# Moving the expansion and mask transfers of a weight-reconstruction stage from ScalarE's DMA queue to GpSimd's

## The reference, cut to what matters

```python
n = out_size * in_size                      # 16.8 million samples
p0, p1, p2, p3 = (control_points[idx[k]] for k in range(4))
w = 0.5 * (2*p1 + (p2-p0)*f + (2*p0-5*p1+4*p2-p3)*f2 + (3*p1-p0-3*p2+p3)*f3)
x = x + ln(attention(ln(x)))
x = x + ln((silu(ln(x) @ gate_w.T) * (ln(x) @ up_w.T)) @ down_w.T)
```

## Time and profile before

| | us |
|---|---|
| two runs | 5064.02 and 5133.34 |
| median of the runs | 5098.68 |
| the profiled execution | 5075.81 |
| span of its slowest core (core 0) | 5074.2 |
| spans of the eight cores | 5041.0 to 5074.2 |

### The profile page before, as it was taken

The page is one execution under the profiler, slowest core; times in us unless marked ns, Lnnn a source line. Parts: engine busy times, 40 slices in busy tenths (PEclk is TensorE's granted clock), DMA queues, the critical chain, the costliest instruction groups (busy, mean ns, idle before and its releaser), DMA issues.

```text
span 5074.2 us, 41718 instructions; the slowest of 8 cores (5041.0 to 5074.2 us)
## 1 busy us (share of the span) xinstructions
PE 2958.4 (58%) x12832; PEld 1170.5 (23%) x12832; DVE 1440.0 (28%) x1876; ACT 924.6 (18%) x1519; POOL 135.0 (3%) x232
## 2 busy tenths in 40 slices
PE   1222222222599996766783122223999893999996
PEld 0000000001244441111131000001444332444332
DVE  3333333335422223444315433333101003010002
ACT  2222222222100003333321122221000002000001
POOL 0000000000000000000000000000000000000000
PEclk9999999999999997777786555556999996999998
DMA  4444444444454431000044799885444344444344
GB/s 94 108 107 110 109 107 110 106 109 128 96 78 77 80 64 51 25 25 25 25 67 141 101 115 115 118 119 130 155 153 150 110 134 137 166 153 154 112 133 145
DMA packets 589352, 538.44 MB, mean 106 GB/s; under 512 B 287152, under 2 KB 502192, under 8 KB 578608
## 3 DMA queue, kind: packets, MB, share of 16 engines
q1 hardware_dynamic: 484816, 397.55, 28.0%
q10 hardware_dynamic: 30464, 83.92, 8.6%
q0 software_dynamic: 73856, 54.30, 8.5%
HBM read 405.40 MB, written 134.22 MB: 106 GB/s over the span
## 4 chain that ended last, share of the span: by engine, by line
PE 46%; ACTq 16%; DVE 15%; DMA 12%; ACT 5%; issue 4%; DVEq 0%; SPq 0%; POOL 0%; POOLq 0%
ACTq L160 16%; PE pq L689 11%; PE pgE L1081 9%; PE puE L1087 9%; DMA di<-dct 5%; PE pdE L1130 5%; DMA wdsb<-wbuf_d 5%; DVE gwo L443 4%; PE pav L226 2%; PE prow L222 2%; ACT gwo L438 2%; PE po L903 2%; PE psc L824 2%; DVE rs L859 2%; PE pguA L422 2%
## 5 line engine op out<-in xcount | busy, mean ns | idle before, releaser
L422 PE MATMUL pguA<-Ug,atsb 16*128 16x512 bf16 x512 | 267.7, 598 | 930.5 <-DVE Ug L387 858.9
L1081 PE MATMUL pgE<-x2f,wgsb 128*128 128x512 bf16 x2048 | 778.6, 380 | 13.6 <-DMA wusb<-wbuf_u 13.6
L1087 PE MATMUL puE<-x2f,wusb 128*128 128x512 bf16 x2048 | 778.5, 380 | 0.0
L443 DVE CAST_PREDICATED gwo<-gm,pguA 128x512 bf16<-128x512 uint8 x512 | 353.6, 691 | 744.0 <-ACT gwo L438 702.8
L689 PE MATMUL pq<-x2T,wq 128*128 128x512 bf16 x2560 | 554.9, 380 | 14.5 <-DMA wq<-wqkvT 14.4
L1130 PE MATMUL pdE<-actsb,wdsb 128*128 128x512 bf16 x2048 | 460.9, 381 | 58.9 <-DMA wdsb<-wbuf_d 58.2
L551 PE MATMUL pdnA<-Ud,atsb 16*128 16x512 bf16 x256 | 133.8, 598 | 563.0 <-DVE Ud L519 528.4
L438 ACT CAST gwo<-pguB 128x512 bf16<-128x512 f32 x512 | 299.6, 585 | 877.7 <-issue 620.7
L689 PEld LDWEIGHTS pq<-x2T,wq 128*128 128x128 bf16 x2560 | 250.3, 98 | 318.8 <-issue 19.3
L1102 DVE TENSOR_TENSOR actsb<-silsb,puE 128x512 bf16<-128x512 bf16 x128 | 88.0, 688 | 815.6 <-ACT silsb L1097 815.6
L422 PEld LDWEIGHTS pguA<-Ug,atsb 16*128 16x128 bf16 x512 | 56.6, 111 | 1134.3 <-issue 1134.3
(11 more groups left out here) (78 smaller groups left out, 1988.5 us busy)
## 6 DMA issues: line engine op xcount, KB each, us to landing
wgsb<-wbuf_g SPq DMA_DIRECT2D x128, 512.0 KB, 3.4
wusb<-wbuf_u SPq DMA_DIRECT2D x128, 512.0 KB, 4.3
wdsb<-wbuf_d SPq DMA_DIRECT2D x128, 512.0 KB, 3.8
gi<-gct ACTq DMA_DIRECT2D x512, 64.0 KB
wbuf_g<-gwo SPq DMA_DIRECT2D x64, 512.0 KB, 5.4
wbuf_u<-gwo SPq DMA_DIRECT2D x64, 512.0 KB, 4.4
wbuf_d<-dwo SPq DMA_DIRECT2D x32, 1024.0 KB, 17.4
wq<-wqkvT POOLq DMA_DIRECT2D x24, 1024.0 KB, 10.5
```

The lines of the kernel that those rows point to most:

```text
L422: t.matmul(pp[:, :], at_sb[u_:u_ + 16, :], U[b][u_:u_ + 16, cc:cc + 512], start=True, stop=True, tile_position=(u_, 0)))
L443: v.copy_predicated(o_, m_, pp[:, :]))
L1081: t.matmul(pg[bi][:, :], wg[o % 4][:, h * 128:h * 128 + 128], x2f[:, h * 512:h * 512 + 512], start=(h == 0), stop=(h == 15)))
L1087: t.matmul(pu[bi][:, :], wu[o % 4][:, h * 128:h * 128 + 128], x2f[:, h * 512:h * 512 + 512], start=(h == 0), stop=(h == 15)))
```

## The change

Every DMA that ScalarE issued in the two weight stages is issued by GpSimd: the expansions, and the mask loads. Their waits move with them. Nothing else is changed: buffers, emission order and sizes stay. GpSimd then gets with chunk c, in this order: two loads of c+2 (waiting for the expansion of c-1), the expansion of c+1 (waiting for its loads and for the product of c-1), the mask load of c+2 (waiting for the last eviction of c-2). That is 11 DMAs a chunk in the gate/up stage and 7 in the down stage. The diff, cut to the gate/up stage; the down stage is changed in the same way:

```diff
                 def expand(c):
-                    sch.wait("S", ltok[c])
+                    sch.wait("G", ltok[c])
                     if c >= 2:
-                        sch.wait("S", umark[c - 2])
+                        sch.wait("G", umark[c - 2])
                     else:
-                        sch.wait("S", msmk_gu)
+                        sch.wait("G", msmk_gu)
                     for si in range(4):
                         wt, dlt = si // 2, si % 2
-                        sch.dma("S", AP(IN0[c % 2], (si * 32) * GCH,
+                        sch.dma("G", AP(IN0[c % 2], (si * 32) * GCH,
                                         [[GCH, 16], [1, GCH]]),
                                 AP(CT[c % 3], (wt * 5 + dlt) * GCH,
                                    [[GCH, 4], [0, 4], [1, GCH]]),
                                 f"we{c % 2}")
                         etok[c] = sch.dma(
-                            "S", AP(IN1[c % 2], (si * 32) * GCH,
+                            "G", AP(IN1[c % 2], (si * 32) * GCH,
                                     [[GCH, 16], [1, GCH]]),
                             AP(CT[c % 3], (10 + dlt * 16) * GCH,
                                [[GCH, 16], [1, GCH]]),
...
                         for cpre in (0, 1):
                             mtoks[cpre] = sch.dma(
-                                "S", MSK[cpre % 4][:, :],
+                                "G", MSK[cpre % 4][:, :],
...
                         if c >= 2:
-                            sch.wait("S", evmark[(c - 2) * 8 + 7])
+                            sch.wait("G", evmark[(c - 2) * 8 + 7])
                         mtoks[c + 2] = sch.dma(
-                            "S", MSK[(c + 2) % 4][:, :],
+                            "G", MSK[(c + 2) % 4][:, :],
```

More of the change, by code:

```diff
@@ L496, in expand @@
                 def expand(c):
-                    sch.wait("S", ltok[c])
+                    sch.wait("G", ltok[c])
                     if c >= 2:
-                        sch.wait("S", umark[c - 2])
+                        sch.wait("G", umark[c - 2])
                     else:
-                        sch.wait("S", msmk_dn)
+                        sch.wait("G", msmk_dn)
                     for si in range(2):
-                        sch.dma("S", AP(IN0[c % 2], (si * 32) * DCH,
+                        sch.dma("G", AP(IN0[c % 2], (si * 32) * DCH,
                                         [[DCH, 16], [1, DCH]]),
@@ L508, in expand @@
                         etok[c] = sch.dma(
-                            "S", AP(IN1[c % 2], (si * 32) * DCH,
+                            "G", AP(IN1[c % 2], (si * 32) * DCH,
                                     [[DCH, 16], [1, DCH]]),
@@ L582, in gen @@
                         if c >= 2:
-                            sch.wait("S", evmark[(c - 2) * NCG + NCG - 1])
+                            sch.wait("G", evmark[(c - 2) * NCG + NCG - 1])
                         mtoks[c + 2] = sch.dma(
-                            "S", MSK[(c + 2) % 4][:, :],
+                            "G", MSK[(c + 2) % 4][:, :],
                             wgm_dn_d[:, (c + 2) * DCH:(c + 3) * DCH],
```

## The result

The changed kernel takes 4499.24 us (median of 11 runs) against 5071.36 us (median of 10 runs of the kernel before beside it): a ratio of 0.8857, interval 0.8826 to 0.8888. The forecast was 4314 us with a range of 4200 to 4620. So the sign was right and the time lies inside the range, but a quarter of the gain that was forecast did not come. The profiled execution took 4489.5 us, 586 less than the one before.

The account below looks back on a forecast made before the run. ScalarE's DMA issuing was taken to hold up its copies and, through them, VectorE and TensorE, with busy transfers beside it in the down stage. Gains of 556 (gate/up) and 206 us (down) from 5075.8 gave 4314 us, range 4200 to 4620.

Parts of the forecast that it names:

- The chain of the gate/up stage: Gate/up: without ScalarE's issuing, VectorE's chain sets a floor of 9.27 us; 9.8 instead of 18.62 a chunk gains 556 us.
- The bounds for the rate of expansions: Gate/up: from 9.27 us a chunk, hidden by the floor, to 12.5 if one expansion must end before the next begins.
- the head start: Expansions start two chunks before they are due; 18.4 us of lead covers the 11.3 us latency of a gate/up expansion.
- the four DMA engines of the shape 4 x 4: Expansion transfers: four of eight are slow because an outermost dimension of 4 uses only 4 of 16 DMA engines.
- GpSimd's price: GpSimd's queue: 0.51 us a DMA, making 5.6 us a gate/up chunk and 3.6 a down chunk, both hidden.
- Both rivals of a dear GpSimd DMA: GpSimd's queue: 1.14 us a DMA binds gate/up (4484 us, chance 0.07); 2 us or more makes it slower (5538 us, 0.04).
- the rival that had GpSimd's queue as the bound: Gate/up: at 1.14 us a DMA GpSimd's queue takes 12.5 us a chunk; 4484 us in all, chance 0.07.
- The down stage's term: Down stage: a chunk takes 14.0 us instead of 20.64, a gain of 206 us.
- 14.0, the middle of the two shares: Down stage: DMA time allows 12.4 us a chunk at share 1.46 or 15.4 at 1.18; 14.0 was taken.
- a share of about 0.95 is all that is to be had, 19.2: Down stage: the upper bound, 19.2 us a chunk if the DMA share can reach only about 0.95.
- The edits at no cost: Outside the chunk chains: first product some us sooner or later, nothing touched behind the barrier, nothing charged for VectorE beside GpSimd's issuing.
- The rival of expansions in line: Both stages: expansions do not overlap; gate/up 11.3 to 12.5 us a chunk, down 16 to 19.2; some 4550 us, chance 0.25.

Follow-up runs that it names:

- e2: Changed kernel with each expansion held on GpSimd's queue until VectorE's fourth eviction of the chunk (fifth in the down stage); 5176.6 us.
- e4: Changed kernel with IN0 transfers reading rows 0, 4, 8, 12 instead of 0, 1, 2, 3, each four times (weights not the reference's); 4373.9 us.
- e5: Kernel before, all on ScalarE's queue, with IN0 transfers reading rows 0, 4, 8, 12 instead of 0, 1, 2, 3 (weights not the reference's); 4681.4 us.
- e1: Changed kernel with only the gate/up stage changed, the down stage as in the kernel before; 4536.59 us, ratio to before 0.8956.

## Why the prediction was right, and where it wasn't

**The chain of the gate/up stage** was read rightly: the floor of 9.27 us is the 9.28 of the timeline, and the forecast of 9.8 stands against 10.07. The term of 556 us measured 539. The bounds for the rate of expansions (9.27 to 12.5) held. That expansions of two chunks may overlap was right: in e2 one takes 11.6 us to its product, more than a whole chunk of the changed kernel.

**What the gain consists of** was told with the wrong weight. I began with ScalarE's copies standing behind its own issuing and treated the head start as what covers the latency. In e2 the first without the second is worth 0.5 us a gate/up chunk as measured, some 2.9 of the 8.55 by the estimate that allows for its later hold, and less than nothing in the down stage either way.

**Why the transfers are slow** was read into the rows. The earlier trace rows give the shortest, the median and the longest issue, and not that four of eight are slow, or which. Nor did the four DMA engines of the shape 4 x 4 turn out to be the main cause: e4 keeps that shape and brings the gate/up chunk to the floor, on GpSimd's queue, and from 18.62 to 14.76 us on ScalarE's (e5). It was the rows that are read.

**GpSimd's price** of 0.51 us a DMA measured 0.54 for expansions, 0.56 for masks of 128 rows and 0.52 for loads. It was busy for 532 us (forecast 510) and was never the bound. Both rivals of a dear GpSimd DMA fell. The time alone would have misled here: 4495 is within 11 us of the rival that had GpSimd's queue as the bound (4484), whose price of 1.14 us is twice the measured one.

**The down stage's term was mis-sized:** 206 us forecast, 88 measured, and 54 with head and drain. The range of 4200 to 4620 was wide enough to hold that error; it had been drawn for other ones. The step that failed is the one that took "14.0, the middle of the two shares". It treated the DMA share as one pool in which any transfer takes the place of any other, and looked only at how soon an expansion lands. I wrote that VectorE would wait for di. It does so for 31.9 us, and ScalarE for 305.2 on stores. The row that bore on it, the store of 1 MB in runs of 128 bytes with 17.4 us to land, was on the page and not in my sum. The case "a share of about 0.95 is all that is to be had, 19.2" is nearest to what came, for another reason.

**The edits at no cost** were not all free: with two expansions and the next loads in flight at once, the first one of the down stage took 21.6 us instead of 13.1 (15.1 in e2, where the second is held), and the stores that are behind must drain before the barrier. "Behind the barrier nothing is touched" was true of the feed-forward stage (1592.6 us against 1593.6), but not of the wait in front of it, nor quite of what lies between the two weight stages, 8.4 us longer.

**VectorE beside GpSimd's issuing** cost nothing, as taken: the product keeps its 1.226 us and the masked copy its 0.691 with GpSimd busy for more than half of the stage.

**The rival of expansions in line** (4550) had the down stage's size about right (16 to 19.2) and its cause wrong; in the gate/up stage it fell.

## What to carry to other kernels

When a compute engine's queue is full of DMA issues, ask first when those DMAs could start, and only then what the issuing costs: here the earlier start carried most of the gain, and the same move with the start held back gave none of it (e2; by estimate less than a quarter with the start at its old place). Before moving issues to another queue, look whether they are slow because of what they read: reading rows four apart instead of four neighbouring ones was worth 121 us of the changed kernel (e4), where the down stage's whole move brought 42 (e1). And price a faster stream by what shares the DMA engines with it: a store in short runs fell far behind beside transfers in large packets, so look for the transfer with the smallest packets and ask who waits for it.

## What the runs showed of the hardware that I had not expected

- The issue of a DMA on ScalarE's queue is not a fixed price: eight transfers of 64 KB took 9.88 us when they read neighbouring rows and 6.22 us when they read rows four apart. From GpSimd's queue both take 0.54 us each; there, what is slow shows in the landing instead (median 6.0 and 3.8 us).
- A store in 128-byte runs moved 952 packets a microsecond in 10 us without GpSimd's transfers; beside them it moved 437 in one stretch and 138 in the next, and its median landing went from 17.4 to 43.9 us.
- A mean DMA share is no measure of room: the down stage kept 0.99 in the changed kernel at 17.81 us a chunk, and e4 had 1.18 at 16.27.
- A stationary operand read with a step of 8 elements loads in 145 ns instead of 98.
